# Key products moved into the projection stage as small tiles, and the block inverses shared between VectorE and GpSimd

## The reference

```
q, v = x @ Wq, x @ Wv ; k = rope(l2norm(x @ Wk)) ; beta = 2 * sigmoid(x @ Wb)     # 16 heads of 16
per chunk:  A  = tril((K K^T) * beta, -1)
            Vn = solve_triangular(eye + A, V - K S)          # S: the state carried along
            S  = S + (K * beta)^T Vn
```

## Time and profile before

| what | us |
|---|---|
| median of three runs | 991.86 |
| lowest, highest | 989.54, 999.53 |
| the profiled execution's own time | 987.09 |
| its span | 985.4 |
| block stage: TensorE's first key product to the scan's first product | 104.0 to 193.25 |

### The profile page before, as it was taken

The page is one execution under the profiler, slowest core; times in us unless marked ns, Lnnn a source line. Parts: engine busy times, 40 slices in busy tenths (PEclk is TensorE's granted clock), DMA queues, the critical chain, the costliest instruction groups (busy, mean ns, idle before and its releaser), DMA issues. The chain is left out here.

```text
span 985.4 us, 23672 instructions
## 1 busy us (share of the span) xinstructions
PE 834.9 (85%) x9023; PEld 590.4 (60%) x9023; DVE 602.9 (61%) x2051; ACT 458.6 (47%) x1082; POOL 285.5 (29%) x533
## 2 busy tenths in 40 slices
PE   6894843688889999989998889959899999997784
PEld 3563733677766666668894455534466666586362
DVE  1786589277778999735434535440389999384264
ACT  2564521100017777743335775563257777564054
POOL 0772230275633333310003100000033333511535
PEclk9996556799979999998988998969789999996798
DMA  6044562333410730030001000000000000290561
GB/s 131 1 107 85 150 187 87 98 94 95 98 25 2 211 93 1 3 97 2 1 1 29 0 0 1 1 1 0 1 1 2 2 3 2 59 282 21 209 228 48
DMA packets 54904, 60.55 MB, mean 61 GB/s; under 512 B 9129, under 2 KB 40327, under 8 KB 54536
## 3 DMA queue, kind: packets, MB, share of 16 engines
q1 hardware_dynamic: 45768, 47.46, 17.9%
q10 hardware_dynamic: 6640, 5.27, 1.9%
q0 software_dynamic: 2384, 6.31, 1.7%
HBM read 29.75 MB, written 25.99 MB: 57 GB/s over the span
## 5 line engine op out<-in xcount | busy, mean ns | idle before, releaser
L905 DVE CUSTOM_DVE_ANT_0 l_masked_scores<-psum,mask_q_rows 128x384 bf16<-128x384 f32 (+3 forms) x512 | 220.6, 487 | 31.0 <-PE psum L845 27.4
L921 ACT ACTIVATE kT_or_probs<-psum 128x512 f32<-128x512 f32 (+1 forms) x192 | 87.2, 529 | 115.4 <-PE psum L831 114.2
L934 POOL TENSOR_SCALAR_AFFINE_SELECT l_probs<-l_probs 128x256 f32<-128x256 f32 x128 | 50.5, 407 | 227.5 <-ACT l_probs L921 227.3
L921 ACT ACTIVATE l_probs<-psum 128x512 f32<-128x512 f32 (+1 forms) x192 | 87.1, 529 | 33.1 <-PE psum L831 31.9
L845 PE MATMUL psum<-l_k_heads,l_q_heads 32*128 32x512 f32 (+3 forms) x512 | 93.8, 485 | 2.4 <-PEq L46 1.5
L845 PE MATMUL psum<-kb_heads,q_heads 32*128 32x384 f32 (+3 forms) x512 | 93.2, 481 | 1.9 <-DVE l_neg_max_rows L905 1.0
L831 PE MATMUL psum<-l_q_and_max,kb_heads 32*128 32x512 f32 (+3 forms) x512 | 87.9, 460 | 0.7 <-DVE l_q_and_max L911 0.7
L831 PE MATMUL psum<-l_q_and_max,l_k_heads 32*128 32x512 f32 (+3 forms) x512 | 87.8, 459 | 0.7 <-DVE l_q_and_max L911 0.7
L934 POOL TENSOR_SCALAR_AFFINE_SELECT kT_or_probs<-kT_or_probs 128x256 f32<-128x256 f32 x128 | 50.5, 406 | 95.1 <-ACT kT_or_probs L921 95.0
L845 PEld LDWEIGHTS psum<-l_k_heads,l_q_heads 32*128 32x128 f32 x512 | 57.6, 196 | 10.2 <-DVE l_neg_max_rows L905 3.8
L678 POOL TENSOR_TENSOR v_new_and_ones<-v_and_k_rows_or_heads 32x128 f32<-32x128 f32 x128 | 55.1, 447 | 27.0 <-DVE v_and_k_rows_or_heads L656 20.7
(11 more groups left out here) (359 smaller groups left out, 1821.1 us busy)
## 6 DMA issues: line engine op xcount, KB each, us to landing
sorted_scratch<-l1p_zeros SPq DMA_DIRECT2D x23, 257.0 KB, 6.3
gram_scratch<-rows_32k SPq DMA_DIRECT2D x4, 1024.0 KB, 4.9
rows_32k<-v_new_and_ones SPq DMA_DIRECT2D x64, 64.0 KB, 2.5
x_rows<-in_L_attn_x_dram SPq DMA_DIRECT2D x16, 128.0 KB, 6.7
heads_scratch<-rows_32k SPq DMA_DIRECT2D x2, 1024.0 KB, 5.4
heads_scratch<-q_kb_T SPq DMA_DIRECT2D x2, 1024.0 KB, 5.9
inverse_scratch<-block_inv SPq DMA_DIRECT2D x2, 1024.0 KB, 4.0
q_heads<-heads_scratch SPq DMA_DIRECT2D x8, 256.0 KB, 3.5
```

Of the source, the lines that this page charges most:

```text
L905: last = self.nc.vector.tensor_tensor_reduce(out=self.junk[:, n % 4, o:o + w], in0=self.g.ps[:, self.row_bank(G, u, i), o:o + w], in1=self ...
L921: self.nc.scalar.activation(self.PT[:, G % 2, 2 * (u % 2) + i, o:o + w], self.g.ps[:, self.e_bank(G, u, i), 0:w], ACT.Exp, scale=SCALE).th ...
L934: last = self.nc.gpsimd.affine_select(out=d, in_=d, pattern=[[0, 2], [1, P]], compare_op=ALU.is_ge, fill=0.0, base=0, channel_multiplier=-1)
```

## The change

Three things move. The key products are formed inside the projection stage, each as four products of 32 x 32 on the batches' own squares (gram, 1024 products instead of 256), in four groups of four chunks between the last transposes, and ScalarE copies whole banks out (gram_rows; of the last group VectorE copies half). The stores to gram_scratch and the loads of beta are issued in the projection stage too. In the block stage all 16 heads' blocks are loaded before either half is solved. Of each eight heads VectorE takes six and GpSimd two (scale_A and substitute, called once by either engine for each half). ScalarE clears the targets of the inverses in GpSimd's place.

```diff
@@ phase_qkv
-        w = sb("l0_wqkvb", [P, KD, WC])
+        w_xT = sb("l0_wqkvb_and_xT", [P, KD * WC + G4 * KD * P])
...
+        AT = [g.kt_or_probs[:, HG * NT * P:], w_xT[:, 0:4 * 2 * D], g.rows32k[:, 0:4 * 2 * D], g.rows32k[:, 4 * 2 * D:8 * 2 * D]]
...
+        def gram_rows(copy, q, j):
+            return copy(AT[q].rearrange("p (f k j m) -> p j k f m", f=2, k=G4 * HG, j=4)[:, j, :, :, :], ps[:, j, :].rearrange("p (k f m) -> p k f m", f=2, m=CH))
+
+        def store_gram(eng, q):
+            dst = bass.AP(tensor=g.gram_d.tensor, offset=g.gram_d.offset + q * G4 * D, ap=[[2 * NT * D, P], [NT * D, 2], [1, G4 * D]])
+            eng.dma_start(dst, AT[q].rearrange("p (f n) -> p f n", f=2)).then_inc(g.gram_st[q], 16)
@@ sync
                 if q == LAST:
...
+                    for n in range(LAST):
+                        sp.wait_ge(at_ok[0], 4 * (n + 1))
+                        store_gram(sp, n)
+                    sp.wait_ge(g.beta_st, 16)
...
@@ scalar
+                if NT < c < NT + 4:
+                    act.wait_ge(gram_ps, c - NT)
+                    if c == NT + 3:
+                        act.wait_ge(kn_ok, LAST)
+                    for n in range(4):
+                        gram_rows(nc.scalar.copy, c - NT - 1, n).then_inc(at_ok[0], 1)
+            act.wait_ge(gram_ps, NG)
+            for n in range(2):
+                gram_rows(nc.scalar.copy, LAST, n).then_inc(at_ok[0], 1)
+            act.wait_ge(at_ok[0], 4 * LAST + 2)
+            act.wait_ge(at_ok[1], 2)
+            store_gram(act, LAST)
             act.wait_ge(kk_sb, 2 * G4 * NG)
             for j in (2, 3):
                 store_heads(act, LAST, 1, SLOT * j + HD, HD)
@@ vector
+            dve.wait_ge(gram_ps, NG)
+            for n in range(2, 4):
+                gram_rows(nc.vector.tensor_copy, LAST, n).then_inc(at_ok[1], 1)
@@ tensor
+            def gram(q):
+                pe.wait_ge(kk_sb, 2 * G4 * (q + 1))
...
+                    pe.wait_ge(at_ok[0], 4 * q)
+                for c in range(G4):
+                    for x in range(HG):
+                        o = (HG * c + x) * R
+                        for b in range(B):
+                            for j in range(4):
+                                kt = g.KT[SLOT * j:SLOT * j + HD, x, G4 * q + c, R * b:R * b + R]
+                                last = nc.tensor.matmul(ps[R * b:R * b + R, j, o:o + R], kt, kt, start=True, stop=True)
+                last.then_inc(gram_ps, 1)
...
+                if c == NT + 3:
+                    k_heads(c - KLAG)
+                    gram(c - NT - 1)
                 if QLAG <= c < NT + QLAG:
                     q_heads(c - QLAG)
-                if KLAG <= c:
+                if KLAG <= c and c != NT + 3:
                     k_heads(c - KLAG)
+                if c in (NT + 1, NT + 2):
+                    gram(c - NT - 1)
+            gram(LAST)
@@ delta_blocks
-        H2 = H // 2
...
+        H2, HV = H // 2, 6
...
+        def scale_A(engine, x, h0, h1, done):
+            for j in range(0, CH, 4):
+                lj = L[:, j:j + 4, H2 * x + h0:H2 * x + h1, j + 1:]
+                engine.tensor_tensor(lj, lj, bcast(bl[:, j:j + 4, H2 * x + h0:H2 * x + h1], [[H, 4], [1, h1 - h0], [0, CH - 1 - j]]), ALU.mult).then_inc(done, 1)
+
+        def substitute(eng, engine, x, h0, h1, room, done):
+            nh = h1 - h0
+            for j in range(CH - 1):
+                n_m, n_i = j + 1, CH - 1 - j
...
+                if j or x:
+                    eng.wait_ge(done, STEPS * x + 2 * j)
+                engine.tensor_tensor(t, a, tj, ALU.mult).then_inc(done, 1)
+                eng.wait_ge(done, STEPS * x + 2 * j + 1)
+                engine.tensor_tensor(ti, ti, t, ALU.subtract).then_inc(done, 1)
...
+        def load_blocks(eng, b0):
+            for c0, c1 in ((0, NT - G4), (NT - G4, NT)):
+                for q in range(c0 // G4, c1 // G4):
+                    eng.wait_ge(g.gram_st[q], 16)
+                for b in (b0, b0 + 1):
+                    for hf in range(2):
+                        p0 = 2 * NT * b + hf
+                        src = bass.AP(tensor=g.gram_d.tensor, offset=g.gram_d.offset + ((R * b + CH * hf) * 2 + hf) * NT * D + c0 * D, ap=[[D, c1 - c0], [2 * NT * D, CH], [1, D]])
+                        eng.dma_start(L[p0 + 2 * c0:p0 + 2 * c1 - 1:2, :, :, :].rearrange("p j h i -> p j (h i)"), src).then_inc(l_ok, 16)
@@ vector
-            for u in range(2 * NP):
-                dve.wait_ge(gram_ps, u + 1)
...
-                for b in range(2):
-                    diagonal(nc.vector.tensor_copy, u, b).then_inc(at_ok[0], 1)
...
+            dve.wait_ge(g.bl_ok, 16 * 2 * B)
+            dve.wait_ge(l_ok, 16 * 4 * B)
             for x in range(2):
+                scale_A(nc.vector, x, 0, HV, la_ok[0])
...
+                substitute(dve, nc.vector, x, 0, HV, tmp, t_step[0])
@@ scalar
+            for i in range(2):
+                heads_stored(act, g, i)
+            load_blocks(act, 2)
+            for x in range(2):
+                nc.scalar.activation(g.rows32k[:, 4 * P * H2 * x:4 * P * H2 * (x + 1)], bcast(g.idf[:, :], [[0, 4 * H2], [1, P]]), ACT.Copy, scale=0.0).then_inc(td_zero, 1)
@@ gpsimd
-            for x in range(2):
-                for i in range(2):
-                    pool.wait_ge(gram_st[2 * x + i], 16)
-                nc.gpsimd.memset(g.rows32k[:, 4 * P * H2 * x:4 * P * H2 * (x + 1)], 0.0).then_inc(td_zero, 1)
             pool.wait_ge(ld, 32)
...
+            pool.wait_ge(g.bl_ok, 16 * 2 * B)
+            pool.wait_ge(l_ok, 16 * 4 * B)
+            for x in range(2):
+                scale_A(nc.gpsimd, x, HV, H2, la_ok[1])
+                pool.wait_ge(la_ok[1], CH // 4 * (x + 1))
+                substitute(pool, nc.gpsimd, x, HV, H2, tmp2, t_step[1])
+            for i in range(2):
+                pool.wait_ge(t_step[i], 2 * STEPS)
+            nc.gpsimd.memset(L[:, :, :, :], 0.0).then_inc(l_zero, 1)
@@ sync
             for i in range(2):
                 heads_stored(sp, g, i)
+            load_blocks(sp, 0)
...
             for x in range(2):
-                sp.wait_ge(t_step, STEPS * (x + 1))
+                for i in range(2):
+                    sp.wait_ge(t_step[i], STEPS * (x + 1))
```

110 lines of the change are left out of this document (31 added, 79 removed).

## The result

The changed kernel takes 1037.46 us in the median of four runs (1034.93 to 1042.16), the kernel before 993.32 us (989.54 to 999.53) beside it: a ratio of 1.0444, 95% interval 1.0374 to 1.0513. It is slower by 44 us. The forecast was 1016 with a range of 989 to 1036: the sign was right, the size was not, and the time lies just outside the range.

The account below looks back on a forecast made before the run. The path was taken as last squares copied (TensorE-bound), VectorE's solve, then tail. Terms +4.8 + 16.2 + 5.3 = +26.3 us on 987.09 gave 1013.4, or 1018 from the median; stated 1016, range 989 to 1036.

Parts of the forecast that it names:

- The key products, 18 ns a record: Projection stage: 512 trace records a group, two per product, 9.5 us a group; last squares copied 4.8 us later.
- 26 ns a record: Rival for the key products: records spaced as in a long row of 64; +16.4 us, 1032; chance 16%.
- 25 ns rule: Key products: starts never closer than about 25 ns; a group an estimated 12.8 us, the sum 14.4 us later.
- The clock at 0.50: Key products in the projection stage: TensorE would be granted half the clock, 0.50.
- The ladder: Projection stage's end: transposes and copies for chunks 12 to 15 would take 11.9 us, before 10.8.
- 7.4 us of unhidden copies: Projection stage: bank copies that, with 38 us of products, replace the block stage's 29 us of products.
- Store and load, +16.2: Between last squares and solve: last store, heads and block loads, no longer hidden, put the solve's start at 155.5; +16.2 us.
- The rival of 7%: Before the solve: late chain constants or 16 loads, 2 MB at once, hold it up some 8 us more; 1024; 7%.
- The solve, +5.3: Block stage: VectorE and GpSimd exclude one another, so their times add; 43.0 us for 37.66, +5.3 us.
- to 0.8 us: Sign in the solve: VectorE's rows of 378 elements would stretch from about 0.55 to 0.8 us.
- The tail, 21.06: From the solve's end to the scan's first product: would keep its 21.06 us.
- The sixteen squares at once: Rival for the key products: all sixteen squares run together, a group 2.0 us instead of 9.5; 986; chance 17%.

Follow-up runs that it names:

- experiment 3: Changed kernel with each small key product streaming 64 columns instead of 32, as many instructions, values not the reference's; span 1044.3 us, +6.8.
- Experiment 6: Changed kernel with block loads issued as one of 16 chunks per batch and half, not 12 then 4; loads 10.5 us for 15.6, one run 1034.9 us.
- experiment 8: Changed kernel without VectorE's six heads of the solve, GpSimd's two alone; their solve took 28.9 us, against 37.44 with both engines.
- experiment 12: Kernel before with four products of the identity on all 128 rows ahead of each unit of key products; 1026.47 us, ratio 1.0344.

## Why the prediction was wrong, step by step

- **The key products, 18 ns a record: the step that failed.** "A group costs 512 x 0.018 = 9.2 us and 0.3 for the last one's own length, 9.5." The groups took 12.6 to 16.1, 58.4 us for 38, so this term was +26.2 and not +4.8. I looked for the price of a record between issue and streaming, from rows of 16 and 64 records, and wrote myself that 512 stand in a row here. Neither row is long enough to show the supply; what pointed to it was the queue table's instruction line, with its 16 KB a packet, which I did not read. What the runs showed in place of one price for a record: 10 ns inside a burst, below my lower bound of 14, then a wait for the next block of 128 pairs, together 28.5 ns a record over the four groups. The rival "26 ns a record" gave 1032 and came near by luck, since its mechanism, streaming, is not the one: experiment 3 doubled the streaming and added 1.0 us to 58.4. The 25 ns rule of the Trainium skill that I weighed (TensorE: Matmul & The Clock Gate) would have given a group of 12.8 us, near the 12.6 of the first, for a reason that the bursts at 10 ns contradict.
- **The clock at 0.50**: right for the products. **The ladder** for the last chunks: 11.1 us (134.12 to 145.25) for 11.9; its last two sets of key transposes took 0.63 us each and not 1.06, at a granted clock of 1.00 (windows at 141.5 and 143.4). The "7.4 us of unhidden copies" of the prediction is not what the sum holds (twice 2.45 and 1.4, 6.3). The last squares were copied 21.4 us later than the 139.3 of the sum, and the products are 20.3 of these.
- **Store and load, +16.2**: the order of events was right, and the size was +23.2. The heads landed 7.5 us after the last squares (7.2 forecast). The loads took 15.6 for 9.0: I took landing times of loads that ran on all engines, and did not see that the change's 4-chunk loads would run on few. Experiment 6 takes 5.1 of the 6.6 away. The rival of 7%, 16 loads that hold the solve up some 8 us more, had this wait nearly in size, with the amount of data as its reason; the same data in eight loads took 10.5.
- **The solve, +5.3**: mechanism right, size wrong, 37.44 for 43.0. The terms at fault are probably GpSimd's two. Alone, its 30 elements take 0.24 us and its 126 take 0.42 (experiment 8), 1.7 to 1.9 ns an element and not 2.1, which is an estimated 1.2 to 2.4 of the 5.6 us. The rest, over 68 instructions, would bring its fixed time under exclusion from 0.1 down to about 0.04 us, just under the bounds of 0.05 to 0.185; how the 5.6 us divide is not shown. The long rows gave the exclusion of the elements and said nothing of the fixed part. The "to 0.8 us" that I named as a sign did not come either: 0.62.
- **The tail, 21.06**: 20.56, right.
- **Not in the sum**: +3.5 us behind the scan's start.
- **The sixteen squares at once** (17%, 986): the record price of 10 ns in bursts lies between that rival and mine, and does not decide, because the supply does. The rival, too, left out how the instructions come.
- Errors were +21.4, +7.0, -5.6, -0.5 and +3.5: 25.8 us on a sum of 26.3. By the medians the loss is 44.1 us, 18 over that sum: the profiled execution before, 987.09, was quicker than all four timed runs, the one after, 1039.2, slower than its median. The miss against the stated 1016 is 21.5.

## What to carry to other kernels

Cutting a product into smaller tiles multiplies instructions, and here TensorE's instructions came in blocks of 128 pairs every 3.3 to 4 us, later when data shared the DMA engines: count pairs in a row, and if they would run in under 26 to 31 ns each, price them at that, not at what a short burst shows. Work that moves ahead of a barrier takes its stores and loads with it; look at what they were hidden under before, and give every load a slowest dimension of 16 pieces (experiment 6: 5.1 us). Don't split two-input work in SBUF between VectorE and GpSimd for its elements: six heads to two saved 0.5 us of 37.9, and no other split was run.

## What the runs showed of the hardware that I had not expected

- The instruction supply: packets of 16 KB, 256 instructions, a burst of 128 records; bursts start 3.28 to 4.0 us apart with idle DMA engines and up to 5.9 under stores.
- Inside a burst the records of 32 x 32 products of float32 start 10 ns apart at a granted clock of 0.50.
- A VectorE step of 378 elements takes 0.55 us alone and 0.62 beside GpSimd; GpSimd's of 120 takes 0.42 alone and 0.62 beside VectorE.
- Loads of 4 pieces moved 96 GB/s at a DMA share of 0.27, loads of 12 moved 166 to 262 GB/s at 0.77 to 0.82, loads of 16 up to 279 GB/s at 0.95 to 1.12.
- 64 us of unbroken work on TensorE, half of it on the full array, left the clock at 1.2 GHz (experiment 12).
